# A mixture-of-experts kernel on one core: where the down products, their weighing and the turning of the next tokens stand in the experts' loop

## The reference, cut to what matters

```python
h = xf @ W_router + b_router
Sm = softmax(h)                              # 8192 tokens x 32 experts
G_ek, idx_ek = top_k(Sm.T, 256)              # each expert takes its 256 best tokens
tokens = xf[idx_ek]
up = einsum('gjkh,ghf->gjkf', tokens, W_up) + b_up      # 128 -> 341, shared by groups of 4 experts
Eout = einsum('ekf,efh->ekh', silu(up), W_down) + b_down
y = zeros.at[idx_ek].add(G_ek[..., None] * Eout)
```

## Time and profile before

| what | us |
|---|---|
| median of 3 runs | 1272.03 (1272.02 to 1273.53) |
| the profiled execution's own time | 1269.29 |
| its span in the profile | 1267.5 |
| busy: PE, DVE, ACT, POOL | 1064.4, 830.8, 678.1, 733.8 |
| experts' loop, first round's count to the last scatter | 1031.6 to 1260.6 |

### The profile page before, as it was taken

One profiled execution on the slowest core, in us unless ns is written; L12 is line 12 of the kernel. 1 busy time (PEld: TensorE's weight loads), 2 busy tenths in 40 slices (PEclk: granted clock), 3 DMA queues, 4 the chain that ended last, 5 costly groups with the idle time before them and its releaser, 6 DMA issues. The chain is left out here.

```text
span 1267.5 us, 23241 instructions
## 1 busy us (share of the span) xinstructions
PE 1064.4 (84%) x7477; PEld 938.4 (74%) x7477; DVE 830.8 (66%) x2691; ACT 678.1 (53%) x1749; POOL 733.8 (58%) x1188
## 2 busy tenths in 40 slices
PE   4679999999999999999999999999982267777661
PEld 3569888988988988998898899888871145555451
DVE  5346777787676867877686777876765765654110
ACT  0346756666665665666566566666553534423220
POOL 5356675676476557646655774444441044677774
PEclk9799999999999999999999999999995566789786
DMA  3011001100010101001110110000002012344442
GB/s 101 19 32 26 22 21 32 30 27 26 10 32 26 33 24 32 26 10 28 30 33 12 42 28 10 11 9 20 11 20 67 0 41 51 69 70 84 86 67 23
DMA packets 49084, 42.62 MB, mean 34 GB/s; under 512 B 6728, under 2 KB 44488, under 8 KB 48840
## 3 DMA queue, kind: packets, MB, share of 16 engines
q0 software_dynamic: 18432, 22.04, 9.4%
q1 hardware_dynamic: 30536, 19.13, 5.0%
HBM read 27.51 MB, written 13.63 MB: 32 GB/s over the span
## 5 line engine op out<-in xcount | busy, mean ns | idle before, releaser
L657 PE MATMUL mixed<-v,pT 128*128 128x131 f32 x2560 | 318.8, 276 | 6.6 <-DVE o L920 3.8
L657 PEld LDWEIGHTS mixed<-v,pT 128*128 128x128 f32 x2560 | 300.8, 190 | 9.7 <-issue 6.7
L913 DVE TENSOR_REDUCE neg_max<-scores 128x1 f32<-128x1024 f32 (+1 forms) x192 | 198.8, 1035 | 48.5 <-PE scores L444 48.4
L1150 POOL DMA_INDIRECT gram<-in_emb,ids x192 | 190.1, 990 | 67.7 <-issue 51.2
L1078 ACT ACTIVATE probs<-scores,neg_max 128x1024 f32<-128x1024 f32 (+1 forms) x192 | 186.2, 970 | 46.7 <-DVE neg_max L913 45.1
L1087 ACT ACTIVATE pT<-turned 128x512 f32<-128x512 f32 x219 | 130.0, 593 | 73.5 <-PE turned L638 72.2
L1201 POOL TENSOR_TENSOR zb<-row,gate 128x384 f32<-128x384 f32 x64 | 54.5, 852 | 149.4 <-DVE gate L948 148.5
L638 PE MATMUL turned<-con,probs 128*128 128x128 f32 x876 | 126.6, 274 | 12.7 <-ACT probs L1078 5.8
L1962 POOL DMA_INDIRECT out_h<-yw,slots x64 | 102.4, 1600 | 53.4 <-DVE yw L1811 27.6
L638 PEld LDWEIGHTS turned<-con,probs 128*128 128x128 f32 x876 | 101.0, 141 | 28.6 <-ACT probs L1078 12.6
L1953 POOL DMA_INDIRECT xg<-token_table,slots x64 | 64.6, 1009 | 72.4 <-DVE slots L1791 53.5
(11 more groups left out here) (348 smaller groups left out, 2526.2 us busy)
## 6 DMA issues: line engine op xcount, KB each, us to landing
wd<-in_w_down SPq DMA_DIRECT2D x32, 171.0 KB
token_table<-w SPq DMA_DIRECT2D x16, 320.0 KB
out_h<-h SPq DMA_DIRECT2D x16, 256.0 KB, 2.3
gram<-in_emb,ids POOLq DMA_INDIRECT x192
wu<-in_w_up SPq DMA_DIRECT2D x8, 170.5 KB
w<-in_weights SPq DMA_DIRECT2D x1, 1174.0 KB
xg<-token_table,slots POOLq DMA_INDIRECT x64
out_h<-yw,slots POOLq DMA_INDIRECT x64
```

The lines of the kernel that those rows point to most:

```text
L657: last = pe.matmul(mixed[:, 0:C + 3], pT[:, n % 2, j * P:(j + 1) * P], vals[:, 0:C + 3], start=(j == 0), stop=(last_half and j == half * 4 ...
L913: dve.tensor_reduce(neg_max[:, n % 4:n % 4 + 1], scores[:, (n % 2) * S:(n % 2) * S + width], AX_X, ALU.max, negate=True).then_inc(maxed, 1)
L1150: pool.indirect_dma_start(gram[:, t % 4, g, :], None, emb[g], bass.IndirectOffsetOnAxis(ap=ids[:, s, t, g:g + 1], axis=0)).then_inc(gather ...
```

## The change

Within the loop, iteration e:

- PE: down(e) comes first, then round 1's total, rank, up(e+1), rows_before, round 2's total, turn(e+2), sums, rows, places, round 3's total.
- DVE: weigh(e) comes right behind count 1, ahead of settle 1; copy_x(e+2) comes behind settle 2, ahead of find_rows and count 3.
- ACT: count 2 comes ahead of silu(e+1).
- Groups 2 and 4 have their places in bank 0 and group 3 in bank 1 (it was the other way round), and the waits that keep them from tokens and sums shift by one iteration: the sums of iteration e wait for weigh(e) and no longer for weigh(e-1) alone; down(e+1), not down(e), waits for the kept sums; turn(e+3), not turn(e+2), waits for the chosen.

```diff
-    PLACE_BANK = (2, 3, 1, 0, 1)
+    PLACE_BANK = (2, 3, 0, 1, 0)
@@ sums(g)
-                    pe.wait_ge(y_v, e)
+                    pe.wait_ge(y_v, e + 1)
@@ places_within(g)
-                    pe.wait_ge(xt_v, e + 1)
+                    pe.wait_ge(xt_v, e + 2)
@@ turn(e)
-            if e - 2 in IN_LOOP:
-                pe.wait_ge(chosen_ok, IN_LOOP[e - 2] + 1)
+            if e - 3 in IN_LOOP:
+                pe.wait_ge(chosen_ok, IN_LOOP[e - 3] + 1)
@@ down(e)
-            if e in IN_LOOP:
-                pe.wait_ge(sums_a, IN_LOOP[e] + 1)
+            if e - 1 in IN_LOOP:
+                pe.wait_ge(sums_a, IN_LOOP[e - 1] + 1)
@@ TensorE's loop
         for e in range(NE):
+            down(e)
+            totals(rounds_of(e)[0:1])
             if e in TRIPLE_AT:
                 rank(TRIPLE_AT[e])
             if e + 1 < NE:
                 up(e + 1)
             if e in TRIPLE_AT:
                 rows_before(TRIPLE_AT[e])
-            totals(rounds_of(e)[0:1])
+            totals(rounds_of(e)[1:2])
+            if e + 2 < NE:
+                turn(e + 2)
             if e in IN_LOOP:
                 sums(IN_LOOP[e])
-            down(e)
-            totals(rounds_of(e)[1:2])
@@
             if e in IN_LOOP:
                 places_within(IN_LOOP[e])
                 places_before(IN_LOOP[e])
-            if e + 2 < NE:
-                turn(e + 2)
             totals(rounds_of(e)[2:])
@@ VectorE's loop
             later_count(first)
+            weigh(e)
             later_settle(first)
             later_count(second)
             if e in TRIPLE_AT:
                 reach(TRIPLE_AT[e])
-            weigh(e)
             later_settle(second)
+            if e + 2 < NE:
+                copy_x(e + 2)
             if e in TRIPLE_AT:
                 find_rows(TRIPLE_AT[e])
             later_count(third)
             if e in IN_LOOP:
                 choose(IN_LOOP[e])
-            if e + 2 < NE:
-                copy_x(e + 2)
             later_settle(third)
@@ ScalarE's loop
                 keep_ranks(TRIPLE_AT[e])
+            later_count(rounds_of(e)[1:2])
             if e + 1 < NE:
                 silu(e + 1)
             if e in IN_LOOP:
                 keep_sums(IN_LOOP[e])
-            later_count(rounds_of(e)[1:2])
```

## The result

The changed kernel takes 1263.9 us (median of 5 runs, 1259.66 to 1269.93) against 1272.03 (5 runs, 1269.87 to 1273.53); the ratio is 0.9948, with a 95% interval of 0.9924 to 0.9972. Seven more runs gave 1261.59 against 1271.14, ratio 0.9931 (0.9904 to 0.9958).

A forecast was written before the change was run, and what follows sets the result against it. POOL's scatter and gather queue was taken to set the end once expert 10's rows arrive; 3.0 us from an earlier weigh(10) plus 1.1 from earlier T saved 4.1 off the median 1272.03, giving 1267.9 us, range 1265.8 to 1272.5.

The forecast's parts named there:

- part 1: Iteration 10: down goes first behind the thresholds, so weigh(10) and expert 10's scatter come 3.0 us earlier with T unmoved.
- T: End of the third settle of the iteration before; for iteration 10 it was forecast to come 1.1 us earlier.
- iteration 0: Down(0) and weigh(0) fit in front of the stalled first settle, taking weigh from in front of settle 2: -0.5 us.
- iteration 1: Down no longer stands behind sums and kept sums, transposes run beside the sums: -1.8 us from 10.87 us.
- iteration 2: Treated as an ordinary iteration, products swapping places; one of six ordinary iterations summing to +0.4 us, its share +0.1.
- iterations 3 and 6: Triple iterations: reach begins later behind both products, while weigh leaves the path: +0.6 and +0.2 us, together +0.8.
- iterations 4, 5, 7, 8, 9: Ordinary iterations: products swap, copy_x stands ahead of count 3; between -0.15 and +0.4 us each, +0.3 together.
- part 3: From expert 10's scatter to the last, POOL's queue keeps the lead; late slots cost 0 to 0.8 us, taken as 0.
- The first (longer circle): Rival: weigh and copy_x lengthen the rounds' circle, T 2 to 3 us later, about 1270.4 us; chance 0.27 with late slots.
- the third (slower by the low level): Rival: new gaps keep PE's clock low in iterations 3 to 9, T 7.7 us later, 1275.6 us; chance 0.12.
- The second, larger gain: Rival: iteration 0's stall falls elsewhere or products run more at the high level, 1266.0 to 1266.9 us; chance 0.13.
- cap of 6.0: Limit on the gain: POOL's queue behind expert 7's scatter allows expert 10's scatter no earlier than 1117.9 us.

The follow-up runs named there:

- before_again: The kernel before the change, unedited, run once more for a second trace; 1269.98 us in a single run.
- turn_early_only: The kernel before with only turn(e+2) and copy_x(e+2) moved early and the banks and waits changed; 1268.6 us, ratio 0.9986.
- down_first_only: The changed kernel with transposes and copy_x back at their old places, down first and ACT's swap kept; 1263.12 us, ratio 0.9938.
- after_filled: The changed kernel with unused matmuls in TensorE's idle time: 8 ahead of round 3's total outside iteration 1, 5 ahead of row lookup; 1254.87 us, ratio 0.9886.
- before_filled: The kernel before with unused matmuls: 8 ahead of round 3's total outside iteration 1, 5 ahead of row lookup; 1266.58 us, ratio 0.9977.
- after_warm0: The changed kernel with 24 unused matmuls ahead of round 3's total in iteration 0 only; 1261.36 us in a single run.
- after_filled_more: The changed kernel with more unused matmuls, sized to TensorE's idle gaps, 24 of them in iteration 0, 19 ahead of the loop; 1251.2 us, ratio 0.9847.
- before_warm0: The kernel before with 24 unused matmuls ahead of round 3's total in iteration 0 only; 1265.94 us in a single run.

## Why the prediction was wrong

Half of the mechanism was right: POOL's queue sets the end, the lead of expert 10's scatter is what counts, and it is made of part 1 and of T. What failed is the step that held the level of TensorE's clock fixed in the sum and let a change of it only cost time. By terms, in us, for the first and the second pair of traces (the forecast's +0.4 for six iterations is split here):

| term | predicted | first traces | second traces |
|---|---|---|---|
| part 1, weigh(10) against T | -3.0 | -3.00 | -4.33 |
| iteration 0 | -0.5 | +0.45 | +0.59 |
| iteration 1 | -1.8 | -3.63 | -2.11 |
| iteration 2 | +0.1 | -2.63 | -1.63 |
| iterations 3 and 6 | +0.8 | +0.37 - 0.28 | -0.34 + 0.39 |
| iterations 4, 5, 7, 8, 9 | +0.3 | +0.98 | +1.00 |
| part 3, scatter 10 to the last | 0 | -1.07 | -1.05 |
| sum | -4.1 | -8.81 | -7.48 |

**Part 1** came out as worked in the first pair, with the down product low (2.93) and DVE's masks ending 0.2 us before it. That it fits to the hundredth is luck as well: it needed the down product of iteration 10 of before to be high (1.58). In before_again it was low (2.90), and the term was 1.3 us larger.

**Iterations 1 and 2: the failed step.** I priced iteration 1 by the low level (2.90) on both sides, and iteration 2 as an ordinary one whose products take what they took. The order's own worth in iteration 1 was undersized: 2.1 to 2.5 us by the runs, where I had 1.8. The rest of the first pair's surplus, 1.1 us there and all 2.6 in iteration 2, is the level of TensorE's clock. In the second pair the level gives nothing in iteration 1, 1.6 us in iteration 2 (products of 2.57 and 2.10 against 1.58 and 1.53) and 1.3 in part 1. I had the level as a rival with a price in one direction only, as a loss, because I looked at the new gap behind the transposes and not at how much of the old order's time was already spent at the low level. That the level is worth this much is shown by the fillers, which leave order and work as they are and take 2.4 to 4.9 us from iterations 0 to 9 of before (82.18 and 84.63 to 79.75) and 6.9 and 10.2 from those of after (79.9 to 73.0 and 69.7).

Why the level is high in iteration 2 of the changed kernel stays open. The two waits that the change takes out of iteration 1 (1.03 us for the kept sums, of which 0.38 is left, and 0.95 for choose) are an obvious guess, but they didn't make the level fall: in the first trace of before it had fallen in iteration 0, 6.0 us behind the loop's start, and iteration 1's first product, ahead of both waits, already took 2.91. In before_again the level rose in the middle of iteration 1 although PE waited there for both, 1.06 and 1.58 us. They may have kept it from returning. For that speaks that iteration 2 took 5.44 to 5.74 in five of the traces of the changed order, and 5.60 in turn_early_only, which still waits 1.04 us for the kept sums but not for choose; it took 6.48 in down_first_only, which still waits for choose, and 7.07 to 8.11 in the four of the old order. Against it: with ACT's old order, where both waits are gone too but PE waits 1.83 us for ACT's count, it ran wholly low (2.90 and 2.89; 9.83 us). And where the level changes fall against the loop differs between executions of the same code, as said above. No run takes the two waits out and leaves the rest.

**Iteration 0.** I kept the stall of 2.61 us and expected down(0) and weigh(0) in its shadow. But DVE halts at the same moment, until 3.3 to 3.6 us behind the loop's start in all twelve traces, on whatever instruction stands there: now weigh, which then has its 0.61 still to do ahead of the settle.

```profile
1040.98 2.90 PE L1623 MATMUL mixed<-wd,hid 114*128 114x128 f32 x12 [0.98 <-issue]
1040.99 0.80 DVE L1691 TENSOR_SCALAR_CACHE_REDUCE below<-v,cand 128x576 bf16<-128x576 f32 x1
...
1044.48 0.61 DVE L1811 TENSOR_SCALAR yw<-mixed,xg 128x128 f32<-128x128 f32 x2 [2.68 <-PE mixed L1623]
```

The down product ended at 1043.88 and weigh began 0.60 later, where it was 0.04 in iteration 10; in after_filled, with the product at 1.58 and done 1.8 us before, weigh was held 2.55 us and the trace says remote. Iteration 0 came out at +0.45 instead of -0.5. The halt is there in either order, 2.5 to 2.7 us of idling each time. The Trainium skill, "Runtime: NRT & Kernel Launch", section "Instruction fetch mechanics", holds that fetching is mostly hidden when instructions follow in order; the trace neither bears that out nor contradicts it here, since no run shows what this halt is.

**Ordinary and triple iterations.** Iteration 5 took 6.82 against 6.9 worked and 7.07 before. Iteration 8, which I gave +0.4, took 6.81 against 5.52, with its products mixed now and both high before; the two traces of before have 5.52 and 7.08 there. At a level that is high on both sides (before_filled, after_filled) the swap costs 0.2 us in iterations 5 and 8, and gains 0.4 to 0.5 in iterations 3 and 6, where I had a loss of 0.6 and 0.2: the loss by weigh and copy_x on the circle was overrated there. So most of the +1.3 us of iteration 8 is the level, this time against the change.

**Part 3.** The gap closed further down the queue: before, three scatters in mid-loop waited 0.45, 0.56 and 0.76 us beyond the usual 0.30 for the landing of the one ahead; after, none did; in the second traces it was the same, with four gaps of 0.60 to 0.70 us before and none after. The slots cost 0.14, and the gather behind them took 1.76. Why the landings came sooner I didn't test.

**Rivals.** The first (longer circle) and the third (slower by the low level) didn't happen. The second, larger gain, was the outcome, and its cap of 6.0 was no cap: it had expert 7's scatter gain 3.4, which gained 7.9 (62.52 us behind the loop's start, 70.39 before), since iterations 1 and 2 lie ahead of it. It did name products at the high level as a way to a larger gain, with a chance of 0.13, but priced only by that cap.

**The median.** I subtracted from the median what I worked out on one profiled execution. The loops' difference by trace (7.5 to 8.8) is what the medians show (8.1 and 9.6), although the two profiled executions themselves differ by 0.6 us the other way.

## What to carry to other kernels

Where TensorE works in bursts, write its clock level into the sum with both signs: products can also come to the high level, and in iterations 1 and 2 of the first pair of traces that was 3.7 of 8.8 us, of which 1.1 was lost again in iteration 8. Take two traces of each kernel before you price it, since the same code met the level differently (iteration 1: 10.87 and 9.35 us). Idle time of TensorE that can't be removed can be filled with unused matmuls (here it took 2.4 to 4.9 us of 82 to 85 on the old order, and up to 10.2 of 80 on the new one). Compare a stretch of two traces by its own first and last events: code ahead of it can move by as much as the change is worth. And when an operation is moved behind a wait on one engine, its partners on others have to move too: ACT's silu left in its old place turned a gain of 0.5 to 0.7% into a loss of 1.3%.

## What the runs showed of the hardware

- The granted clock stayed at 0.50 through 6 us in which TensorE was busy without a gap (1042 to 1048 in after_filled), after about 2 us of near idleness; the next 2 us were at 0.91. With 24 fillers in that idle time instead of 8, the products behind it ran at the high level in both kernels of the new order (after_warm0, after_filled_more: 1.58 and 1.53); on the old order (before_warm0) the first one still took 2.66.
- Equal code lands on different levels in different executions: the kernel before took 10.87 and 9.35 us in iteration 1 and 5.52 and 7.08 in iteration 8. The two traces of the changed kernel agree to hundredths of a us (iterations 1, 2, 5 and 8: 7.24, 5.44, 6.82, 6.81 each time), with the level rising at nearly the same offset in both (4.5 and 4.7 us).
- A halt of DVE in iteration 0 (named remote by the profile of before and of after_filled) ends 3.3 to 3.6 us behind the loop's start in either order, whichever instruction it falls on.
- Executions of one kernel differ by up to 13.8 us (before, 22 runs: 1264.0 to 1277.81). Between the first traces of before and after, 8.0 us arose in the first 100 us, in equal code.
